# Gated cross-attention and feed-forward on one core: keys and probabilities are turned by DMA transposes, the high and the low half of each key tile by a transfer each

## What is computed

```python
q = (hidden_states @ Wq).reshape(B, Sq, H, D)           # B 32, Sq 100, H 16, D 128
k = (encoder_hidden_states @ Wk).reshape(B, Skv, H, D)  # Skv 361
v = (encoder_hidden_states @ Wv).reshape(B, Skv, H, D)
q = rmsnorm(q, gq)
k = rmsnorm(k, gk)
scores = jnp.einsum('bqhd,bkhd->bhqk', q, k) * scale
attn = jax.nn.softmax(scores, axis=-1)
out = jnp.einsum('bhqk,bkhd->bqhd', attn, v)
return out.reshape(B, Sq, H * D) @ Wo
...
x = x + jnp.tanh(g_xattn[0]) * xattn(layernorm(x), ctx_1024, ...)
x = x + jnp.tanh(g_ffn[0]) * ffn(layernorm(x), ...)
```

## Time and profile before

| | |
|---|---|
| three timed runs | 2820.04, 2822.2 and 2822.61 us, median 2822.2 |
| the profiled execution | 2822.88 us, of it 2821.1 from the first to the last instruction |
| mean granted TensorE clock | 0.970 of full speed |
| busy PE, DVE, ACT, POOL | 92%, 74%, 62%, 26% of the span |
| DMA | 33 GB/s on the mean over the span |

### The profile page before, as it was taken

One profiled execution on the slowest core, in us unless ns is written; L12 is line 12 of the kernel. 1 busy time (PEld: TensorE's weight loads), 2 busy tenths in 40 slices (PEclk: granted clock), 3 DMA queues, 4 the chain that ended last, 5 costly groups with the idle time before them and its releaser, 6 DMA issues. The chain is left out here.

```text
span 2821.1 us, 60152 instructions
## 1 busy us (share of the span) xinstructions
PE 2586.8 (92%) x19714; PEld 1918.6 (68%) x19866; DVE 2078.7 (74%) x5039; ACT 1757.5 (62%) x4314; POOL 744.0 (26%) x1215
## 2 busy tenths in 40 slices
PE   3799999999999999999999999999999999479998
PEld 2577777777777778677777777777777787344443
DVE  5785868686868686777868686868686868259997
ACT  4675757575757576666757575757575757364443
POOL 3232333232322323232323232323233332000000
PEclk8899999999999999999999999999999999789999
DMA  5101010101010000000010001010101000414444
GB/s 181 38 1 30 2 30 1 30 1 30 2 30 1 11 21 2 30 2 30 2 30 1 30 2 30 2 30 2 30 2 30 1 13 1 166 50 112 112 112 101
DMA packets 96011, 93.84 MB, mean 33 GB/s; under 512 B 56208, under 2 KB 67760, under 8 KB 95152
## 3 DMA queue, kind: packets, MB, share of 16 engines
q1 hardware_dynamic: 95664, 89.44, 10.8%
HBM read 63.21 MB, written 13.11 MB: 27 GB/s over the span
## 5 line engine op out<-in xcount | busy, mean ns | idle before, releaser
L498 ACT ACTIVATE ksq<-keys_ps 128x512 f32<-128x512 f32 (+1 forms) x384 | 229.1, 597 | 516.3 <-PE keys_ps L25 510.6
L868 POOL TENSOR_SCALAR kvar<-kss 128x4 f32<-128x4 f32 (+1 forms) x384 | 79.5, 207 | 1416.8 <-DVE kss L649 1416.8
L871 POOL TENSOR_TENSOR krs<-kvar,minus_half 128x4 f32<-128x4 f32 (+1 forms) x384 | 390.1, 1016 | 32.0
L514 ACT ACTIVATE prob<-score_ps,nbias,qrs 100x361 f32<-100x361 f32 x512 | 336.1, 656 | 43.6 <-DVE nbias L681 43.1
L676 DVE TENSOR_REDUCE nmax<-score_ps 100x1 f32<-100x361 f32 x512 | 270.9, 529 | 104.8 <-PE score_ps L25 99.8
L522 ACT ACTIVATE prob<-prob,rden 100x361 f32<-100x361 f32 x512 | 317.8, 621 | 0.9 <-DVE rden L687 0.9
L657 DVE TENSOR_TENSOR khat<-keys_ps,krs 128x512 f32<-128x512 f32 (+1 forms) x384 | 262.7, 684 | 63.2 <-POOL krs L871 63.2
L24 PE MATMUL keys_ps<-wk_lo,ctxT_hi 128*128 128x512 bf16 (+1 forms) x768 | 299.3, 390 | 9.7 <-issue 2.7
L25 PE MATMUL keys_ps<-wk_hi,ctxT_lo 128*128 128x512 bf16 (+1 forms) x768 | 298.2, 388 | 0.0
L649 DVE TENSOR_REDUCE kss<-ksq 128x4 f32<-128x512 f32 (+1 forms) x384 | 262.5, 683 | 14.7 <-ACT ksq L498 7.8
L23 PE MATMUL shared_ps<-xT_hi,wq_hi 128*128 128x200 bf16 x1024 | 255.9, 250 | 15.0 <-DVE wq_lo L643 14.9
(11 more groups left out here) (153 smaller groups left out, 6418.3 us busy)
## 6 DMA issues: line engine op xcount, KB each, us to landing
ctx_raw<-in_ctx SPq DMA_DIRECT2D x32, 256.0 KB, 3.3
xin<-in_x SPq DMA_DIRECT2D x32, 200.0 KB
xres<-in_x SPq DMA_DIRECT2D x32, 200.0 KB
x_rows<-xres SPq DMA_DIRECT2D x32, 200.0 KB
xin<-x_rows SPq DMA_DIRECT2D x25, 256.0 KB, 2.8
xres<-x_rows SPq DMA_DIRECT2D x25, 256.0 KB, 2.7
out<-xres SPq DMA_DIRECT2D x25, 256.0 KB, 2.8
g_raw<-in_L_ffn_w_gate SPq DMA_DIRECT2D x2, 2048.0 KB, 11.0
```

Source lines behind the costliest of these rows:

```text
L498: act.activation(ksq[0:KV[t], k, :], keys_ps[k][0:KV[t], :], ACT.Square).then_inc(ksq_done, 1)
L514: act.activation(prob[:, v % 2, h, 0:SK], score_ps[h % 2][0:SQ, 0:SK], ACT.Exp, bias=nbias[:, col:col + 1], scale=qrs[:, v // 2 % 2, r:r + 1],
L871: pool.tensor_tensor(krs[0:KV[t], k, :], kvar[0:KV[t], k, :], minus_half[0:KV[t], 0:G], ALU.pow).then_inc(krs_done, 1)
```

## The change

**Halves before turning.** ACT writes the high half of a key tile from `khat` to `ksplit` in SBUF (`keys_hi`), POOL subtracts to the low half (`keys_lo`). For probabilities the ACT instruction that multiplied by 1/sum now writes bf16 into `psplit` (`probs_hi`), and DVE computes the low half from `prob`, the factor and the high half in one instruction (`probs_lo`).

**Turning.** SP issues DMA transposes (`dma_start_transpose`), SBUF to SBUF: for each unit six for the keys (three tiles, high and low, 128 or 112 rows by 512) and two for the probabilities (two heads each, 112 rows by 1536). `turn_ps` and the PE transposes of keys and probabilities are gone, and with them the ACT and DVE instructions that emptied those banks.

**Order.** Units are handled in pairs of turns (`two_turns`). Keys are made two units ahead, not three, and turned in the same turn; the loop starts at turn 1, turn 0 stands ahead of it (`first_turn`). Queries and head outputs are handled two heads at a time (400 columns instead of 200 for ACT and DVE). `project` is spread over the even turns and accumulates in two PSUM banks of its own (`y_ps`), which a matmul with zeros opens.

**Buffers.** `ksplit` and `psplit` are single, `kT`, `pT` and `qT` are double. ACT waits for the transfers of one unit before it writes the halves of the next.

```diff
+            def turn_keys(i, u, t):
+
+                b, rows = u % 2, -(-KV[t] // 16) * 16
+                if t == 0 and started(unit(i, u) - 1):
+                    sp.wait_ge(scored, head(i, u - 1, 0))
+                    sp.sem_inc(sp_passed, 1)
+                for half, done in ((0, k_hi_done), (1, k_lo_done)):
+                    sp.wait_ge(done, tile(i, u, t) + 1)
+                    sp.sem_inc(sp_passed, 1)
+                    sp.dma_start_transpose(kT[:, b, half, :, t * P:t * P + rows],
+                                           ksplit[0:rows, t, half, :]).then_inc(kT_in[b], 16)
+
+            def turn_probs(i, u, k):
+
+                b = u % 2
+                sp.wait_ge(p_lo_done, head(i, u, (k + 1) * TWO))
+                sp.sem_inc(sp_passed, 1)
+                sp.dma_start_transpose(pT[:, b, k, :, :, :, :].rearrange("p a h t q -> p (a h t) q"),
+                                       psplit[:, k, :, :, :].rearrange("q a h s -> q (a h s)")
+                                       ).then_inc(pT_in[b], 16)
...
+                if has_keys(u, last):
+                    turn_keys(i, u + 2, 0), turn_keys(i, u + 2, 1), turn_keys(i, u + 2, 2)
+                if has_scores(u, last):
+                    turn_probs(i, u + 1, 0), turn_probs(i, u + 1, 1)
...
-            def turn_keys(i, u, h):
-
-                n = key_turn(i, u, h)
...
-                for t in range(KVT):
-                    last = pe.transpose(turn_ps[h % 2][:, t * P:t * P + KV[t]],
-                                        khat[0:KV[t], u % 2, t, h * D:(h + 1) * D], ident[0:KV[t], 0:KV[t]])
-                last.then_inc(turned, 1)
...
+                if hg == 0 and m % TWO == 0:
+                    eng.wait_ge(y_added, i * 2 + 1)
+                    pe.matmul(y_ps[m // TWO][:, 0:TWO * QT], zeros[:, :], wk_hi[:, 0, 0:TWO * QT],
+                              start=True, stop=False)
...
+            def keys_hi(i, u, t):
+
+                eng.wait_ge(khat_done, tile(i, u, t) + 1)
+                if t == 0 and started(unit(i, u)):
+                    eng.wait_ge(kT_in[1 - u % 2], keys_turned(i, u - 1))
+                copy(ksplit[0:KV[t], t, 0, :], khat[0:KV[t], (u + t) % 2, :]).then_inc(k_hi_done, 1)
...
+            def probs_hi(i, u, h):
+
+                b = u % 2
+                if h == 0 and started(unit(i, u)):
+                    eng.wait_ge(pT_in[1 - b], probs_turned(i, u - 1))
+                eng.wait_ge(rden_done, head(i, u, h) + 1)
+                act.activation(psplit[0:SQ, h // TWO, 0, h % TWO, 0:SK], prob[:, b, h, :], ACT.Copy,
+                               scale=rden[:, b, h:h + 1]).then_inc(p_hi_done, 1)
...
+            def probs_lo(i, u, h):
+
+                b = u % 2
+                eng.wait_ge(p_hi_done, head(i, u, h) + 1)
+                dve.scalar_tensor_tensor(out=psplit[0:SQ, h // TWO, 1, h % TWO, 0:SK], in0=prob[:, b, h, :],
+                                         scalar=rden[:, b, h:h + 1], in1=psplit[0:SQ, h // TWO, 0, h % TWO, 0:SK],
+                                         op0=ALU.mult, op1=ALU.subtract).then_inc(p_lo_done, 1)
...
+            def keys_lo(i, u, t):
+
+                eng.wait_ge(k_hi_done, tile(i, u, t) + 1)
+                pool.tensor_tensor(ksplit[0:KV[t], t, 1, :], khat[0:KV[t], (u + t) % 2, :], ksplit[0:KV[t], t, 0, :],
+                                   ALU.subtract).then_inc(k_lo_done, 1)
```

More of the change, by code:

```diff
@@ new lines, in shared_uses @@
+        for u in [] if first else range(1, UNITS, 2):
+            v = u + 1
+            if more_queries(u, last):
+                order += [("q", u, 0)]
+            if u == UNITS - 3 and not last:
+                order += [("ctx", 0, 0)]
+            if more_queries(u, last):
+                order += [("q", u, 1)]
+            if u == UNITS - 3 and not last:
+                order += [("ctx", 0, 1)]
+            order += [("m", u, 0), ("m", u, 1)]
+            if u == UNITS - 5 and not last:
+                order += [("x", 0)]
+            if more_queries(u, last):
+                order += [("qss", u)]
+            order += [("o", v, 0), ("o", v, 1)]
+            if u == UNITS - 5 and not last:
+                order += [("x", 1)]
+            if u == UNITS - 3 and not last:
+                order += [("ctx", 1, 0), ("ctx", 1, 1)]
+            if has_mixed(v, last):
+                order += [("m", v, 0), ("m", v, 1)]
@@ new lines, in shared_uses, with has_keys, has_scores, has_mixed @@
+        return order
+    def has_keys(u, last):
+        return u + 2 < UNITS or not last
+    def has_scores(u, last):
+        return u + 1 < UNITS or not last
+    def has_mixed(u, last):
+        return u < UNITS or not last
+    def more_queries(u, last):
+        return u % 2 == 1 and ((u + 3) // 2 < NG or not last)
+    AT_FIRST = {k: n for n, k in enumerate(shared_uses(True, False))}
+    AT_LOOP = {k: n for n, k in enumerate(shared_uses(False, False))}
+    AT_LAST = {k: n for n, k in enumerate(shared_uses(False, True))}
@@ L86, in use, with unit, head, tile @@
         last = isinstance(i, int) and i == PAIRS - 1
[L87 removed]
+        k = (AT_LAST if last else AT_LOOP)[key] + len(AT_FIRST)
         return i * USES + k, k % 2
[L92 to L102 removed]
+    def unit(i, u):
+        return i * UNITS + u
+    def head(i, u, h):
+        return i * (UNITS * G) + (u * G + h)
+    def tile(i, u, t):
+        return i * (UNITS * KVT) + (u * KVT + t)
+    def keys_turned(i, u):
+        return i * (UNITS // 2 * KVT * 32) + (u // 2 + 1) * (KVT * 32)
+    def probs_turned(i, u):
+        return i * (UNITS // 2 * 32) + (u // 2 + 1) * 32
     with ExitStack() as stack:
@@ L256, in _ @@
+            with sp.Fori(0, PAIRS - 1) as i:
+                for u in range(1, UNITS + 1):
+                    turn(i, u, False)
+            for u in range(1, UNITS + 1):
+                turn(PAIRS - 1, u, True)
             for b in range(2):
@@ new lines, in turn_y, with first_turn @@
+            def turn_y(i, b):
+                eng.wait_ge(y_free, (i + 1) * YB)
+                for m in range(NT):
+                    last = pe.transpose(y_ps[b][0:SQ, m * P:(m + 1) * P], yT[:, m, b * SQ:(b + 1) * SQ], ident[:, :])
+                last.then_inc(y_turned, 1)
+            def first_turn(i, u):
+                keys(i, u + 2, 0), keys(i, u + 2, 1)
+                scores(i, u + 1, 0), scores(i, u + 1, 1)
+                keys(i, u + 2, 2)
+                scores(i, u + 1, 2), scores(i, u + 1, 3)
+                mixed(i, u, 0), mixed(i, u, 1)
@@ L504, in turn_probs_hi, with keys_square @@
-            def turn_probs_hi(i, u, h):
-                eng.wait_ge(turned, prob_turn(i, u, h) + 1)
-                copy(pT_hi[:, :, h * SQ:(h + 1) * SQ],
-                     turn_ps[h % 2][:, 0:KVT * SQ].rearrange("p (t q) -> p t q", t=KVT)).then_inc(turn_hi, 1)
+            def keys_square(i, u, t):
+                eng.wait_ge(keys_done, tile(i, u, t) + 1)
+                act.activation(ksq[0:KV[t], (u + t) % 2, :], keys_ps[(u + t) % 2][0:KV[t], :],
+                               ACT.Square).then_inc(ksq_done, 1)
```

1037 lines of the change are left out of this document (548 added, 489 removed).

## The result

| | before | after |
|---|---|---|
| median of the runs | 2822.4 us | 2602.6 us (2601.4 to 2608.0) |
| ratio | | 0.923, 95% interval 0.921 to 0.924 |
| profiled execution | 2822.9 us | 2608.0 us |
| forecast | | 2538 us, range 2490 to 2700 |

The kernel is 7.7% faster, where I had forecast 10%. The time is in the range, at the foot of the rival "waits take part of the gain" (2600 to 2690 us). The profiled execution is 70 us over the forecast.

The account below looks back on a forecast made before the run. The prediction took PE's matmul stream to bound the attention part. From 2822.9 us: -303 for transposes, +5.5 for matmuls with zeros, +13 for new waits, -6 for the prologue, +6 for the last turns gave 2538 us, range 2490 to 2700.

Parts of the forecast that it names:

- waits take part of the gain: Rival: hand-overs between engines and queue come late, one to two waits per two turns, 2600 to 2690 us; chance 0.23.
- PE is the bound, and what leaves it leaves the time: Attention part: PE's stream of matmuls bounds about 2330 us, so a pair goes from 147 to 128 us.
- The price of the transposes: PE in the attention loop: removing key and probability transposes saves 19.0 us a pair, -303 us over 16 pairs.
- DVE, ACT and POOL: Other engines in a pair: 97, 84 and 61 to 77 us, all covered by PE's 128.
- The transfers' landing and the DMA engines: DMA transposes in a turn: key transfers land in 3 us, probabilities in 3.5; DMA share near 0.45.
- transfers that do not overlap: Rival: each transpose occupies the queue until it lands, 34.4 us a turn, 4890 us in all; chance 0.07.
- The transfers' issue: SP's queue in a turn: 5.1 us by size to 15 us fixed; took the former, plus a little, of 16.
- 4 us to spare: Landing of key and probability transfers within two turns: hidden from PE with 4 us to spare each.
- The 0.2 us per two turns for new waits: Tight hand-overs in the loop: 0.2 us charged per two turns, 64 times, +13 us.
- the hand-overs that I named: Head outputs waiting for mixed's second low half, projection waiting for head outputs' low half: half a microsecond of slack.
- the -6: Prologue: one turn more there, one less in the loop, two units of keys instead of three; -6 us (-20 to +10).
- the +6: Last turns: softmax, split and landing of the last unit's probabilities exposed, 3 us to mixed become some 9; +6 us.

Follow-up runs that it names:

- the kernel with a third of them: The kernel before, with one of three PE transposes of each head's keys and probabilities left in the loop, two left out: 2712.7 us, ratio 0.960.
- the experiment with one head more: The changed kernel with one more transfer behind each key transfer, turning the first head of that half again: 3263.5 us, ratio 1.156.

## Why the prediction was right and wrong

- **PE is the bound, and what leaves it leaves the time: right.** The pair shrank by 14.1 us, PE's busy time by 16.6. No other engine came near the pair's length. The price of the transposes was right in size: 18.0 us a pair against 19.0. It holds as a price of a head and not of a single transpose, as the kernel with a third of them shows. The new order of the instructions came together with the transfers; no run has one without the other, so what the order alone gives or takes is not shown.
- **DVE, ACT and POOL: right.** 99, 87 and 74 us against 97, 84 and 61 to 77. `probs_lo` took 0.61 us instead of 0.55, `keys_hi` 0.63 instead of 0.60; POOL's subtraction 1.17, inside 0.67 to 1.34.
- **The transfers' landing and the DMA engines: right.** A key transfer lands in 2.4 us, one of probabilities in 3.6 (forecast: 3 and 3.5), the share is 0.54 (forecast: 0.45). The rival of transfers that do not overlap fell: a turn with eight of them takes 16.6 us, not 34.
- **The transfers' issue: the step that failed.** I bounded SP's time in a turn between 5.1 us (by size) and 15 us (a fixed price) and took the lower end, as if the time of an issue went by size, since the row of 1.87 us was for four times the bytes. The runs show a fixed price: 1.23 us for 32 KB, 1.19 for 128, 1.23 for 256. Eight transfers are 11 us of 16.6. "Either way the turn covers it" was then true on average and false once a pair, because I had counted the queue's transfers alone and not the stores, the wait for them and the loads that it also carries, 9.9 us at one place. The hand-overs of "4 us to spare" could not take that. Price: 2.4 to 3.2 of the 3.6 us a pair that the loop is over the forecast, 33 to 41 us in all; most of the rest is the 1 us by which the transposes were priced too high.
- **The 0.2 us per two turns for new waits: right in sum, wrong in place.** It meant 0.8 us a pair. With the queue's toll taken away PE's idle time is 6.9 us a pair, 0.9 over the kernel before. But it is not spread over the hand-overs that I named: 1.8 us of it stand at one place, a low half behind a row maximum and a scaling on DVE, once a pair.
- **The ends: wrong, with errors that partly cancel.** The first store is 31 us later than meant, the last pair 11 us shorter. The prologue has taken over a turn from the last pair, without the cover of other work; I named the move, but neither the -6 nor the +6 had the time of a turn (16.6 us) in it. The exposed wait that the +6 stood for is there: in the last pair PE stands once for 5.3 us for a transfer of probabilities. Part of what delays the prologue besides is the one thing that I named ("the transposes of two units stand between the loads of weights on SP") and then priced within -20 to +10. Moving the splits gave 10 us back at the first store; the other 20 are not separated into their parts.
- **The rival.** "Waits take part of the gain" gave 2600 to 2690 us for one or two waits of 1.2 us per two turns. The time was there, at its foot, the mechanism only in part: not one or two waits in every two turns, but about one a pair for a late transfer (12 in all, 14.2 us, the longest 2.5), some with a stretch of half clock behind them, and ACT held up by the same queue. The bounds were loose too: 77 and 154 us on a sum without its own 13 us of waits are 2602 and 2679 us.
- **The price per block.** The Trainium skill, page "VectorE: DVE Perf Modes", section on the three transpose paths, gives 1309 ns for one 128x128 bf16 block by DMA. A transfer of one block (32 KB) in the experiment with one head more holds the queue for 1.23 us and lands in 2.4, and one of eight blocks holds it for 1.23 and lands in 3.1. That figure is thus near what a transfer of up to 256 KB costs its queue, and is not a rate per block. Read like that, it would have given 8 x 1.31 = 10.5 us a turn, an estimate close to the 11 us measured, and nearer than my own.

## What to carry to other kernels

Price a DMA queue as an engine: count of transfers times the issue time measured for that kind of transfer (here 1.2 us for a transpose of up to 256 KB), together with everything else that the same queue issues and waits for, and look at the place where these come together, not at the mean of a turn. Splitting a transfer so that its first half can leave early is worth something only if somebody waits for that half; here joining the halves gave back 39 us. When PE gets shorter, a part of the gain comes back as waits for the other engines (here 0.9 of 18 us, in a kernel with fewer transposes 1.6 of 8.7); check each place where a bank is freed by an engine that itself stands behind a third one.

## What was not expected of the hardware

- A DMA transpose from SBUF to SBUF holds SP's queue for 1.19 to 1.23 us between 32 and 256 KB, 1.37 at 336 KB and 1.86 at 512 KB, while its landing goes from 2.4 to 4.3 us. Ordinary loads and stores mostly hold it for 0.3 to 0.4 us.
- Two thirds of the f32 transposes between bf16 products cost PE 0.068 us each, all of them 0.094 each on average. What the first one of a head pays for is not shown by any run here.
- Each start of the loop costs PE 2.0 to 3.0 us for its instruction stream; with three pairs written out, ten starts fewer gave 29 us, 2.9 us each.
- After 2.15 us without work PE had a granted clock of 0.50 for 3.2 us, with 1.00 before and after, so that wait cost more than its own length. It is no fixed price: after 2.65 us without work at the start of another pair the clock was 1.00, and a stretch at 0.50 from 967.0 to 970.4 us had no wait of over 0.4 us in the 3 us before it, in which 16 of the 28 matmuls had one column.
